# Token rows scattered whole by expert pair, loaded back in plain groups, added into the output; layer norm shifts on GpSimd

## The chip, the cores and the metric

The kernel runs on one core of a Trainium2 chip. The metric is the time of one execution on the device in microseconds (us), median of the runs. Engines are TensorE (PE; PEld is its weight load), VectorE (DVE), ScalarE (ACT), GpSimd (POOL) and SyncE (SP), which here only issues DMAs.

## What is computed

A block of adaptive layer norm, an attention-like recurrence with its own feed-forward, then a mixture of 8 experts of which each token takes 2. Eight sequences of 1,024 tokens, 128 channels, float32:

```
mod = (silu(c) @ wmod)  ->  sa, ca, ga, sb, cb, gb   (128 each, per sequence; |ga|, |gb| >= 0.25)
h = layernorm(x) * (1 + ca) + sa
x = x + ga * attn(h)        # rms norm, 5 mixes, 8-key recurrence S = d*S + k*v, o = r.S, ffn
h = layernorm(x) * (1 + cb) + sb
top 2 of softmax(h @ Wg.T), weights scaled to sum 1
x = x + gb * sum_e weight_e * ((a_e * sigmoid(b_e)) @ Wo + bo)   # a_e, b_e = h @ W1[e] + b1[e]
```

The x of the last line is called x2 below, its h is called h3, and gb the gate.

## The kernel before

**First stage** (`attention_block`). 16 tiles of 512 tokens, two to a sequence, go through a software pipeline: `run_pipeline` runs 27 iterations, and in iteration `it` the function `step` of each engine issues the work of tile `it - lag` for lags 0 to 8. `step` is written out by hand, so its order is the order of the engine's queue. VectorE forms `kv`, eight keys a tile, from `v_spread`, a row spread over the partitions by a DMA of 256 KB (L583), scans it (L1287) and GpSimd multiplies the states by r (L708, eight per tile). Layer norms: VectorE makes mean and variance, GpSimd the variance plus epsilon and the power -1/2 (`rs`, L787 and L789 for the second norm, L806 and L823 for the first), VectorE the shift -mean*rs (`mean_shift`, L1278), and ScalarE h*rs + shift.

**Routing.** After each fourth tile a batch of 16 groups of 128 tokens is routed: on VectorE 30 steps of `Router`, spread over the next iterations, find each token's pair of experts (28 classes) and its place `dest` in a list with a region for each class. Per tile SP stores h3 (L608), x2 (L611) and the gate of the sequence, spread over 512 rows (L619), into `tokens_scratch`. Per group GpSimd scatters rows of 16 bytes, the tags (token number and weights), to `list_scratch` at `dest` (L686). The `spot`s of `list_some` say where in an iteration. `list_scratch` was filled with the tag of no token at the start (`clear_list`). Three batches are listed in the first stage, the fourth in the second. Experts' weights come in iteration 21 (L631), when the state products are done, and are split in two halves on ScalarE and VectorE (L1547, 'gel' and 'w_hi' in rows of this part are reused buffers).

**Second stage** (`expert_block`). After a barrier, 91 groups of 128 places, 46 pairs of groups, 20 groups from the first three batches' full blocks (early) and 71 late. Per group SP loads the tags (L1625, L1626), at a row number read from `row_table`; GpSimd gathers the 128 rows of h3, x2 and gate by token number (L1743, five pairs ahead) and scatters the results (L1749). Per pair TensorE transposes h3 (L1644), multiplies by the class's experts, VectorE multiplies by the gate (`gate`, L1818) and adds x2 (`finish`, L1826). The late groups' loads wait for the last batch's listing (`list_late`), which waits for the early groups' loads.

## Time and profile before

| what | us |
|---|---|
| median of 3 runs (lowest, highest) | 815.12 (813.99, 816.86) |
| the profiled execution's own time | 810.64 |
| its span in the trace | 808.8 |
| busy: TensorE / VectorE | 669.2 / 657.2 |
| busy: ScalarE / GpSimd | 474.8 / 613.5 |

The span runs from the first to the last recorded instruction; 1.8 us of the execution lie around it. An engine's busy time is the sum of its instructions' durations; matmul ends are modelled. The first stage ends at 525.96 us in the trace, the second stage begins at 530.51. A tile is counted by the start of its ruk multiply on VectorE (L1430): 128.37, 152.38, 176.46, 201.36, 225.53, 250.31, 280.82, 310.44, 334.61, 363.10, 398.18, 426.10 us.

### The profile page before, as it was taken

How to read it: one execution, taken by the hardware profiler on the slowest of the kernel's cores; microseconds unless marked ns; L12 is line 12 of the kernel's file. 1: busy time of each engine (PE TensorE's matmuls, PEld its weight loads, DVE VectorE, ACT ScalarE, POOL GpSimd, SP SyncE). 2: the span in 40 equal slices, each digit the busy share in tenths (PEclk: the TensorE clock that was granted, in tenths of full speed). 3: DMA queues.
4: the chain of work that ended last, by engine and by line, in shares of the span. 5: the costliest groups of instructions: out<-in, count | busy, mean ns of one | idle time of the engine just before them, and what ended most of it. 6: DMA issues, size and time to landing. Idle time of an engine off the chain costs nothing. (4 is left out here: it accounts for less than half of the span.)

```text
span 808.8 us, 14121 instructions
## 1 busy us (share of the span) xinstructions
PE 669.2 (83%) x3703; PEld 521.4 (64%) x3703; DVE 657.2 (81%) x1426; ACT 474.8 (59%) x1163; POOL 613.5 (76%) x657
## 2 busy tenths in 40 slices
PE   2566899998999789988877967329879999999993
PEld 0444577676777558665655756118668888888882
DVE  5399999999999999979999467707748887788873
ACT  3664789887997678875655655214334444444441
POOL 5377878998998688999779785636777777777763
PEclk7798999999999899998999977559989999999997
DMA  4987767887887867766774262423144433333320
GB/s 125 244 129 139 125 142 132 130 161 131 157 157 125 127 114 133 128 110 115 100 95 94 63 171 64 95 63 84 32 107 104 97 92 95 97 97 96 97 65 1
DMA packets 95298, 89.64 MB, mean 111 GB/s; under 512 B 22832, under 2 KB 71194, under 8 KB 95094
## 3 DMA queue, kind: packets, MB, share of 16 engines
q1 hardware_dynamic: 84438, 66.49, 45.0%
q0 software_dynamic: 10784, 22.25, 9.9%
q8 instruction: 34, 0.56, 0.3%
q14 instruction: 42, 0.34, 0.1%
HBM read 38.69 MB, written 22.41 MB: 76 GB/s over the span
## 5 line engine op out<-in xcount | busy, mean ns | idle before, releaser
L708 POOL TENSOR_TENSOR rs_prod<-rT,state 128x512 f32<-128x512 f32 x128 | 165.2, 1303 | 35.9 <-DVE state L1287 34.0
L1743 POOL DMA_INDIRECT xg<-tokens_scratch,listed x91 | 88.9, 977 | 42.0 <-issue 25.6
L1749 POOL DMA_INDIRECT out<-res,listed x91 | 91.0, 1000 | 34.6 <-issue 25.7
L1282 DVE TENSOR_TENSOR kv<-key,v_spread 128x512 f32<-128x512 f32 x128 | 84.3, 669 | 10.6 <-DMA v_spread<-vT 9.3
L1713 ACT ACTIVATE sig<-ps_a 128x256 f32<-128x256 f32 x91 | 35.0, 385 | 82.5 <-PE ps_a L1653 69.1
L1287 DVE TENSOR_TENSOR_SCAN state<-decay,state,kv 128x512 f32<-128x512 f32 x64 | 79.9, 1269 | 0.1
L1287 DVE TENSOR_TENSOR_SCAN state<-decay,kv 128x512 f32<-128x512 f32 x64 | 76.0, 1207 | 0.1
L1067 PEld LDWEIGHTS ps_k<-w,gel 128*128 128x128 f32 x512 | 61.0, 199 | 14.7 <-issue 12.5
L1715 ACT ACTIVATE sig<-ps_b 128x256 f32<-128x256 f32 x91 | 35.0, 384 | 51.5 <-PE ps_b L1653 51.5
L1067 PE MATMUL ps_k<-w,gel 128*128 128x128 f32 x512 | 64.0, 285 | 1.2 <-ACT gel L924 1.2
L1790 DVE SCALAR_TENSOR_TENSOR ps_a<-ps_a,listed,sig 128x256 f32<-128x256 f32 x91 | 44.3, 487 | 24.8 <-ACT sig L1713 24.8
L1049 PE MATMUL ps_f<-hnT_hi,mix_hi 128*128 128x512 f32 x128 | 56.4, 440 | 6.5 <-DVE hnT_lo L1411 6.3
L1797 DVE SCALAR_TENSOR_TENSOR half<-ps_b,listed,sig 128x256 f32<-128x256 f32 x91 | 44.0, 483 | 21.8 <-ACT sig L1715 21.4
L686 POOL DMA_INDIRECT list_scratch<-tags,dest x48 | 49.4, 1030 | 11.1 <-issue 9.9
L1051 PE MATMUL ps_f<-hnT_hi,mix_lo 128*128 128x512 f32 x128 | 52.1, 407 | 0.0
L1682 PEld LDWEIGHTS ps_y<-out_w,gT 128*128 128x128 f32 x364 | 47.7, 191 | 6.6 <-issue 1.7
L1050 PE MATMUL ps_f<-hnT_lo,mix_hi 128*128 128x512 f32 x128 | 51.8, 405 | 0.0
L1682 PE MATMUL ps_y<-out_w,gT 128*128 128x128 f32 x364 | 48.2, 275 | 2.2 <-DVE res L1826 1.5
L1034 PE MATMUL ps_o<-rs_prod,reduce_w 128*32 128x512 f32 x256 | 35.8, 633 | 12.9 <-POOL rs_prod L708 12.8
L1650 PE MATMUL ps_a<-bias_all,parts 128*128 x91 | 44.4, 487 | 1.4 <-DVE xT_lo L1785 1.3
L1806 DVE TENSOR_TENSOR glu<-ps_a,half 128x256 f32<-128x256 f32 x91 | 38.2, 419 | 4.3
L1049 PEld LDWEIGHTS ps_f<-hnT_hi,mix_hi 128*128 128x128 f32 x128 | 25.3, 197 | 23.2 <-issue 17.1
(298 smaller groups left out, 2068.4 us busy)
## 6 DMA issues: line engine op xcount, KB each, us to landing
v_spread<-vT SPq DMA_DIRECT2D x128, 256.0 KB, 6.5
xin<-in_L_attn_x SPq DMA_DIRECT2D x16, 256.0 KB, 7.2
tokens_scratch<-mods_scratch SPq DMA_DIRECT2D x16, 256.0 KB, 10.4
x<-in_L_attn_x SPq DMA_DIRECT2D x16, 256.0 KB, 4.8
tokens_scratch<-x SPq DMA_DIRECT2D x16, 256.0 KB, 5.4
tokens_scratch<-h SPq DMA_DIRECT2D x16, 256.0 KB, 4.5
list_scratch<-gel SPq DMA_DIRECT2D x1, 3584.0 KB, 11.9
rs_prod<-in_L_ffn_W SPq DMA_DIRECT2D x8, 256.0 KB, 5.3
```

Of the source, the lines that this page charges most:

```text
L686: pool.indirect_dma_start(list_dram, bass.IndirectOffsetOnAxis(ap=dest[:, g:g + 1], axis=0), tags[:, g, :], None).then_inc(s["listed"], 16)
L708: pool.tensor_tensor(rs_prod[:, p, idx % 4], rT[p][:], state[idx][:, p * NT:(p + 1) * NT], ALU.mult).then_inc(s["rs_ready"], 1)
L1049: pe.matmul(dst[:], mix_hi[:, a, m, :], hnT_hi[p][:, cols_of], start=(a == NOW), stop=False)
L1050: pe.matmul(dst[:], mix_hi[:, a, m, :], hnT_lo[p][:, cols_of], start=False, stop=False)
L1051: mm = pe.matmul(dst[:], mix_lo[:, a, m, :], hnT_hi[p][:, cols_of], start=False, stop=(a == BEFORE))
L1067: mm = pe.matmul(ps_k2[:, q * P:(q + 1) * P], gel[c][:, q * P:(q + 1) * P], w2[:, c, :], start=(c == 0), stop=(c == NF - 1))
L1282: dve.tensor_tensor(kv[idx % 2][:], key[:], v_spread[idx % SPREADS][:], ALU.mult).then_inc(s["kv_ready"], 1)
L1287: dve.tensor_tensor_scan(state[idx][:, 1 + p * NT:1 + (p + 1) * NT], decay[:], kv[idx % 2][:], first, ALU.mult, ALU.add) \
L1650: pe.matmul(dst[:], parts[:], bias, start=True, stop=False)
L1682: mm = pe.matmul(ps_y[:, i * P:(i + 1) * P], gT[k % 2][:, h, i * P:(i + 1) * P], out_w[:, h, :], start=(h == 0), stop=(h == NH2 - 1))
L1743: pool.indirect_dma_start(xg[:, 2 * (k % LOADS) + i, :], None, pay_dram, bass.IndirectOffsetOnAxis(ap=listed[:, j, ID:ID + 1].bitcast(I32) ...
L1749: pool.indirect_dma_start(out_rows, bass.IndirectOffsetOnAxis(ap=listed[:, j, ID:ID + 1].bitcast(I32), axis=0), res[k % RESULTS][:, i, :], ...
```

## The change

* The shift of both layer norms is made on GpSimd: a multiply of the mean by -1, and, behind the power, a multiply by `rs` (both 128x4). VectorE's instruction goes.
* `list_scratch`, its clear and the gates' store go. `sorted_scratch` holds whole rows of 260 floats (h3, gate, tags) by class. For the first two batches SP stages two groups at a time into SBUF (`stage_pair`: h3, gate and tags, three DMAs) and GpSimd scatters them from there (`list_pair`, two scatters at each odd spot, as many as before). For the last two batches the rows lie in `last_rows`, in the memory of the states; `load_last_rows` brings in 3 MB ahead of iteration 20. The third batch's 16 scatters stand at spot 7 in one piece, and the last batch's in the second stage wait for nothing (`list_late`, four a pair).
* x2 is stored to the output, and the second stage's scatter adds to it (`compute_op=ALU.add`); `finish` multiplies by the gate in place of adding x2, and `gate` goes.
* In the second stage SP loads each group's rows itself (`load_group`, no gather). After 12 of them come 28 DMAs that write 128 rows of no token behind the last token of each class (`fill_end`), then the other loads; a pair's loads wait for the results stored six pairs before.
* Wo, the experts' output weights, is loaded in iteration 21 too.

```diff
-    TWO_FOUND, CHOSEN, PLACED, STEPS = 7, 14, 27, 30
+    TWO_FOUND, CHOSEN, TAGGED, PLACED, STEPS = 7, 14, 25, 27, 30
...
-    pay_dram = nc.dram_tensor("tokens_scratch", (TILES * NT + 1, 3 * D), F32, kind="Internal").ap()
-    list_dram = nc.dram_tensor("list_scratch", (CLASSES * STRIDE + P, 4), F32, kind="Internal").ap()
...
+    pay_dram = nc.dram_tensor("tokens_scratch", (EARLY * NT, D), F32, kind="Internal").ap()
+    sorted_dram = nc.dram_tensor("sorted_scratch", (CLASSES * STRIDE + P, ROW), F32, kind="Internal").ap()
...
+        state_rows = keep.enter_context(nc.sbuf_tensor("state_rows", [P, max(DK * (1 + T), 2 * RG * ROW)], F32))
+        last_rows = state_rows[:, 0:2 * RG * ROW].rearrange("p (g c) -> p g c", c=ROW)
...
-                    sp.dma_start(pay_tiles[t, 0], h3[p][:]).then_inc(s["h3_stored"][p], 16)
...
+                        sp.dma_start(pay_tiles[t], h3[p][:]).then_inc(s["h3_stored"][p], 16)
...
+                        sp.dma_start(last_rows[:, (t - early) * NQ + RG:(t - early + 1) * NQ + RG, 0:P], h3[p][:]).then_inc(s["h3_stored"][p], 16)
...
-                    sp.dma_start(pay_tiles[t, 1], x2[p][:]).then_inc(s["x2_stored"][p], 16)
+                    sp.dma_start(out_tiles[t], x2[p][:]).then_inc(s["x2_stored"][p], 16)
...
-                for t, p, b in tile(4):
-                    sp.dma_start(pay_gates[t], mods_dram[b, GB:GB + 1, :].broadcast_to([NT, P])).then_inc(s["gates_stored"], 16)
+                for r in batch(3):
+                    stage_pair(r, 0)
...
                 for t, p, b in tile(3):
                     spread_value(7, t, p)
+                for r in batch(3):
+                    stage_pair(r, 1)
...
+            def stage_pair(r, m):
+
+                if r < LISTED - 1:
+                    first, k = r * RG + 2 * m, m % 2
+                    sp.wait_ge(s["route_step"], r * Router.STEPS + Router.TAGGED)
+                    for p in range(2):
+                        sp.wait_ge(s["h3_stored"][p], 16 * BATCH // 2 * (r + 1))
+                    if r > 0 or m >= 2:
+                        sp.wait_ge(s["listed"][k], 16 * 2 * (r * RG // 4 + m // 2))
+                    sp.dma_start(stage[k][:, :, 0:P], pay_groups[:, first:first + 2, :]).then_inc(s["staged"][k], 16)
+                    sp.dma_start(stage[k][:, :, GATE:TAGS], mods_dram[first * P // (TPB * NT), GB:GB + 1, :].unsqueeze(0).broadcast_to([P, 2, P])) \
+                        .then_inc(s["staged"][k], 16)
+                    sp.dma_start(stage[k][:, :, TAGS:], tags[:, first:first + 2, :]).then_inc(s["staged"][k], 16)
...
+            def load_last_rows():
+
+                sp.wait_ge(s["rs_ready"], TILES * DK)
+                for p in range(2):
+                    sp.wait_ge(s["h3_stored"][p], 16 * (early // 2))
+                sp.dma_start(last_rows[:, 0:RG, 0:P], pay_groups[:, (LISTED - 1) * RG:, :]).then_inc(s["last_staged"], 16)
+                for i in range(2 * BATCH // TPB):
+                    first = i * TPB * NQ
+                    sp.dma_start(last_rows[:, first:first + TPB * NQ, GATE:TAGS],
+                                 mods_dram[early // TPB - BATCH // TPB + i, GB:GB + 1, :].unsqueeze(0).broadcast_to([P, TPB * NQ, P])).then_inc(s["last_staged"], 16)
+
...
+            run_pipeline(step, {CLEAR_AT: store_blank, BIAS_AT + 1: store_bias, ROWS_AT: load_last_rows, EXPERTS_AT: load_experts})
...
+            def list_pair(r, m):
+
+                k = m % 2
+                if r < LISTED - 1:
+                    pool.wait_ge(s["staged"][k], 48 * (r * RG // 4 + m // 2 + 1))
+                    pool.wait_ge(s["route_step"], (r + 1) * Router.STEPS)
+                for n in range(2 * m, 2 * m + 2):
+                    g = r * RG + n
+                    if r < LISTED - 1:
+                        pool.indirect_dma_start(sorted_dram, bass.IndirectOffsetOnAxis(ap=dest[:, g:g + 1], axis=0), stage[k][:, n % 2, :], None).then_inc(s["listed"][k], 16)
+                    else:
+                        pool.indirect_dma_start(sorted_dram, bass.IndirectOffsetOnAxis(ap=dest[:, g:g + 1], axis=0), last_rows[:, n, :], None).then_inc(s["last_listed"], 16)
 
             def list_some(r, spot):
...
+                if r < LISTED - 1 and spot % 2 == 1 and spot <= RG + 1:
+                    list_pair(r, spot // 2 - 1)
+                if r == LISTED - 1 and spot == 7:
+                    pool.wait_ge(s["last_staged"], 16 * (1 + 2 * BATCH // TPB))
+                    pool.wait_ge(s["tags_set"], 1)
+                    pool.wait_ge(s["route_step"], LISTED * Router.STEPS)
+                    for m in range(RG // 2):
+                        list_pair(r, m)
+
+            def mean_shift(dst, rs, done):
+
+                pool.tensor_tensor(dst[:], dst[:], rs[:], ALU.mult).then_inc(done, 1)
...
+                    after(pool, s["xn4_ready"], t - 1)
+                    pool.tensor_scalar(shift4[:], mv4[:, :, 0], -1.0, 0.0, ALU.mult, ALU.add)
                     pool.tensor_scalar(ve4[:], mv4[:, :, 1], 1.0, EPS_LN, ALU.mult, ALU.add).then_inc(s["ln2_ve"], 1)
                     after(pool, s["ln2_ve"], t)
                     pool.tensor_tensor(rs4[:], ve4[:], minus_half[:], ALU.pow).then_inc(s["ln2_rstd"], 1)
+                    after(pool, s["ln2_rstd"], t)
+                    mean_shift(shift4, rs4, s["shift2_ready"])
...
-                    after(dve, s["ln1_rstd"], t)
-                    mean_shift(shift1, mv1, rs1, s["shift1_ready"])
...
+            dve.tensor_copy(end_table[:], off[0:1, :, RG:RG + 1].rearrange("p e g -> p (e g)"))
...
+            def load_group(j):
+                k = j // 2
+                if k >= LOADS and j % 2 == 0:
+                    sp.wait_ge(s["stored"][(k - LOADS) % RESULTS], 16 * count_to(k - LOADS, RESULTS))
+                row = sp.value_load(row_table[0:1, j:j + 1], min_val=0, max_val=CLASSES * STRIDE)
+                sp.dma_start(xg[:, slot(j), :], sorted_dram[bass.ds(row, P), :]).then_inc(s["x_in"][k % LOADS], 16)
+
+            def fill_end(c):
+
+                row = sp.value_load(end_table[0:1, c:c + 1], min_val=0, max_val=CLASSES * STRIDE)
+                sp.dma_start(sorted_dram[bass.ds(row, P), :], sorted_dram[CLASSES * STRIDE:, :]).then_inc(s["filled"], 16)
+
+            for j in range(2 * LOADS):
+                load_group(j)
+                if j == 1:
+                    sp.dma_start(out_b[:], ins["L0_ffn_bo"].unsqueeze(0).broadcast_to([P, P])).then_inc(s["small_in"], 16)
+            for c in range(CLASSES):
+                fill_end(c)
+            for j in range(2 * LOADS, GROUPS):
+                if j == early_groups:
 
                     sp.wait_ge(s["listed"], 16 * RG)
-                load_list(c)
+                    sp.wait_ge(s["filled"], 16 * CLASSES)
+                load_group(j)
...
             def scatter(k, i):
                 j = 2 * k + i
                 pool.wait_ge(s["res_ready"], k + 1)
-                pool.indirect_dma_start(out_rows, bass.IndirectOffsetOnAxis(ap=listed[:, j, ID:ID + 1].bitcast(I32), axis=0), res[k % RESULTS][:, i, :], None,
-                                        bounds_check=TILES * NT - 1, oob_is_err=False).then_inc(s["stored"][k % RESULTS], 16)
+                pool.indirect_dma_start(out_rows, bass.IndirectOffsetOnAxis(ap=share_of(j, ID).bitcast(I32), axis=0), res[k % RESULTS][:, i, :], None,
+                                        bounds_check=TILES * NT - 1, oob_is_err=False, compute_op=ALU.add).then_inc(s["stored"][k % RESULTS], 16)
 
             def list_late(first, end):
...
                     g = LATE_BATCH + n
-                    pool.indirect_dma_start(list_dram, bass.IndirectOffsetOnAxis(ap=dest[:, g:g + 1], axis=0), tags[:, g, :], None).then_inc(s["listed"], 16)
-
...
+                    pool.indirect_dma_start(sorted_dram, bass.IndirectOffsetOnAxis(ap=dest[:, g:g + 1], axis=0), last_rows[:, RG + n, :], None).then_inc(s["listed"], 16)
+
             for k in range(PAIRS):
-                if k + AHEAD < PAIRS:
-                    gather(k + AHEAD, 0)
+                if k < LIST_AT:
+                    list_late(RG * k // LIST_AT, RG * (k + 1) // LIST_AT)
                 if k >= 1:
                     scatter(k - 1, 0)
-                if k + AHEAD < PAIRS and members(k + AHEAD) == 2:
-                    gather(k + AHEAD, 1)
-                if k >= 1:
                     scatter(k - 1, 1)
-                if k < LIST_AT:
-                    list_late(RG * k // LIST_AT, RG * (k + 1) // LIST_AT)
...
+            def finish(k):
...
-                y = ps_y[:, 0:n * P].rearrange("p (i d) -> p i d", i=n)
-                dve.tensor_tensor(y, y, xg[:, slot:slot + n, 2 * P:3 * P], ALU.mult).then_inc(s["gated"], 1)
...
-                dve.wait_ge(s["gated"], k + 1)
...
-                dve.tensor_tensor(res[k % RESULTS][:, 0:n], y, xg[:, slot:slot + n, P:2 * P], ALU.add).then_inc(s["res_ready"], 1)
+                dve.tensor_tensor(res[k % RESULTS][:, 0:n], y, xg[:, first:first + n, GATE:TAGS], ALU.mult).then_inc(s["res_ready"], 1)
```

The order of GpSimd in one listing tile (middle of an iteration; `ve`, `rs` are the norms' scalars, `rs_prod` the state products), before:

```order
L787 TENSOR_SCALAR ve<-mv 128x4
L789 TENSOR_TENSOR rs<-ve,minus_half 128x4
L708 TENSOR_TENSOR rs_prod<-rT,state 128x512
L686 DMA list_scratch<-tags,dest 229504x4
L806 TENSOR_SCALAR ve<-mv 128x4
L708 TENSOR_TENSOR rs_prod<-rT,state 128x512
L686 DMA list_scratch<-tags,dest 229504x4
L823 TENSOR_TENSOR rs<-ve,minus_half 128x4
```

and of the change:

```order
L842 TENSOR_SCALAR shift<-mv 128x4
L843 TENSOR_SCALAR ve<-mv 128x4
L845 TENSOR_TENSOR rs<-ve,minus_half 128x4
L757 TENSOR_TENSOR shift<-shift,rs 128x4
L761 TENSOR_TENSOR rs_prod<-rT,state_rows 128x512
L865 TENSOR_SCALAR shift<-mv 128x4
L866 TENSOR_SCALAR ve<-mv 128x4
L761 TENSOR_TENSOR rs_prod<-rT,state_rows 128x512
L740 DMA sorted_scratch<-stage,dest 233088x260 x2
L883 TENSOR_TENSOR rs<-ve,minus_half 128x4
L757 TENSOR_TENSOR shift<-shift,rs 128x4
```

Four small operations are added per tile, and two scatters stand together where there was one and one.

The order of SP in the same tile, from the store of x2 on, before:

```order
L611 DMA tokens_scratch<-x 128x4x128
L583 DMA v_spread<-vT 128x1x512
L617 DMA x<-in_L_attn_x 128x4x128
L619 DMA tokens_scratch<-mods_scratch 512x128
L583 DMA v_spread<-vT 128x1x512 x3
L516 DMA mods_late<-mods_scratch 128x384
```

and of the change:

```order
L618 DMA out<-x 128x4x128
L586 DMA v_spread<-vT 128x1x512
L624 DMA x<-in_L_attn_x 128x4x128
L656 DMA stage<-tokens_scratch 128x2x128
L657 DMA stage<-mods_scratch 128x2x128
L659 DMA stage<-tags 128x2x4
L586 DMA v_spread<-vT 128x1x512
L656 DMA stage<-tokens_scratch 128x2x128
L657 DMA stage<-mods_scratch 128x2x128
L659 DMA stage<-tags 128x2x4
L586 DMA v_spread<-vT 128x1x512 x2
L523 DMA mods_late<-mods_scratch 128x384
```

Six staging DMAs with their waits stand around the spread of key 7 and ahead of those of keys 0 and 1; the gates' store is gone.

SP in the second stage, one list load before:

```order
L1625 TENSOR_LOAD row_table
L1625 ISA x2
L1626 ISA
L1626 DMA listed<-list_scratch 128x4
```

and of the change the twelfth group load and the first fill:

```order
L1690 ISA
L1690 DMA xg<-sorted_scratch 128x260
L1694 TENSOR_LOAD end_table
L1694 ISA x2
L1695 ISA
L1695 DMA sorted_scratch<-sorted_scratch 16x2080
```

A load or a fill has the same five instructions as a list load had; 28 fills stand between loads 12 and 13.

## Rows read from the trace of the kernel before

**Rows 1.** the page, busy us by engine (share of the span)

```profile
PE 669.2 (83%) x3703; PEld 521.4 (64%) x3703; DVE 657.2 (81%) x1426; ACT 474.8 (59%) x1163; POOL 613.5 (76%) x657
```

**Rows 2.** four stretches: start:end, length, busy PE PEld DVE ACT POOL, clock, DMA, GB/s

```profile
128.40:250.30 121.90, 116.05 (x702) 87.99 (x701) 120.08 (x229) 106.83 (x262) 112.93 (x111) 0.99 0.81 145
250.30:310.40 60.10, 50.12 (x278) 38.12 (x277) 60.00 (x121) 41.38 (x108) 45.68 (x44) 0.91 0.72 119
310.40:440.00 129.60, 110.44 (x641) 81.25 (x639) 123.97 (x217) 91.33 (x219) 112.72 (x107) 0.95 0.69 116
...
598.40:788.20 189.80, 189.80 (x1081) 162.54 (x1080) 152.87 (x397) 86.57 (x216) 143.59 (x145) 1.00 0.36 94
```

**Rows 3.** grouped instructions, 100 to 450 us

```profile
L1278 DVE SCALAR_TENSOR_TENSOR shift<-mv,rs 128x4 f32<-128x4 f32 x23 | 14.3, 621 | 4.2 <-POOL rs L789 4.2
...
L789 POOL TENSOR_TENSOR rs<-ve,minus_half 128x4 f32<-128x4 f32 x12 | 12.3, 1022 | 1.0
...
L787 POOL TENSOR_SCALAR ve<-mv 128x4 f32<-128x4 f32 x12 | 3.0, 249 | 1.0
```

**Rows 4.** GpSimd in order of time, one calm tile (start, length, what)

```profile
201.80 1.29 POOL L757 TENSOR_TENSOR h_all<-h_all,mods_early 128x512 f32<-128x512 f32 x1 [1.34 <-ACT h_all L860]
...
210.44 0.19 POOL L782 TENSOR_SCALAR ve<-ssq 128x4 f32<-128x4 f32 x1 [0.81 <-ACT hn L855]
...
213.06 1.29 POOL L708 TENSOR_TENSOR rs_prod<-rT,state 128x512 f32<-128x512 f32 x1
...
225.78 1.30 POOL L757 TENSOR_TENSOR h_all<-h_all,mods_early 128x512 f32<-128x512 f32 x1
```

**Rows 5.** VectorE in order of time, first stage: waits and shifts

```profile
32.09 0.87 DVE L1267 BATCH_NORM_STATS2 st<-xin 128x6 f32<-128x128 f32 x4 [7.20 <-DMA xin<-in_L_attn_x]
...
213.30 1.07 DVE L1278 SCALAR_TENSOR_TENSOR shift<-mv,rs 128x4 f32<-128x4 f32 x1
...
350.55 1.24 DVE L1278 SCALAR_TENSOR_TENSOR shift<-mv,rs 128x4 f32<-128x4 f32 x1 [4.16 <-POOL rs L789]
```

**Rows 6.** one listing tile in order of time: GpSimd, sync queue, VectorE

```profile
340.18 1.28 POOL L759 TENSOR_TENSOR h_all<-h_all,mods_early 128x512 f32<-128x512 f32 x1
...
341.23 3.46 SPq L583 DMA_DIRECT2D v_spread<-vT  x3
...
356.79 1.26 DVE L1282 TENSOR_TENSOR kv<-key,v_spread 128x512 f32<-128x512 f32 x2
```

**Rows 7.** DMA issues on the page: KB each, us to landing

```profile
v_spread<-vT SPq DMA_DIRECT2D x128, 256.0 KB, 6.5
...
list_scratch<-gel SPq DMA_DIRECT2D x1, 3584.0 KB, 11.9
```

**Rows 8.** all engines in order of time, the first stage's last tiles

```profile
465.76 7.25 SPq L631 DMA_DIRECT2D rs_prod<-in_L_ffn_W  x8
...
468.18 0.96 POOL L686 DMA_INDIRECT list_scratch<-tags,dest  x1 [0.30 <-issue]
...
470.56 1.28 ACT L865 ACTIVATE h<-h_all,rs 128x128 f32<-128x128 f32 x4 [3.28 <-POOL rs L779]
```

**Rows 9.** sync queue and GpSimd at the second stage's start

```profile
530.51 3.73 SPq L1626 DMA_DIRECT2D listed<-list_scratch  x4
...
535.47 17.25 SPq L1626 DMA_DIRECT2D listed<-list_scratch  x16
535.75 0.99 POOL L1743 DMA_INDIRECT xg<-tokens_scratch,listed  x1 [13.53 <-DMA listed<-list_scratch]
```

**Rows 10.** TensorE's transposes of a pair's rows, one row a pair

```profile
540.29 0.66 PE L1644 MATMUL ps_t<-ident,xg 128*128 128x128 f32 x2 [14.90 <-DMA xg<-tokens_scratch,listed]
...
590.89 0.69 PE L1644 MATMUL ps_t<-ident,xg 128*128 128x128 f32 x2 [6.82 <-DMA xg<-tokens_scratch,listed]
...
598.36 0.38 PE L1644 MATMUL ps_t<-ident,xg 128*128 128x128 f32 x2
```

**Rows 11.** grouped instructions, 530.5 us to the end

```profile
L1818 DVE TENSOR_TENSOR ps_y<-ps_y,xg 128x256 f32<-128x256 f32 (+1 forms) x46 | 19.7, 429 | 1.6
```

More of the change, by code:

```diff
@@ L33 @@
 GATE_MIN = 0.25
-ID, LOW, HIGH, BOTH = range(4)
+ID, LOW, HIGH, BOTH, TAG = range(5)
+GATE, TAGS, ROW = P, 2 * P, 2 * P + TAG
 PACK = 1 << 12
```

188 lines of the change are left out of this document (83 added, 105 removed).

## The prediction

> **What bounds the kernel now.** I read the page's busy shares first, then the stretches, then each engine in order of time where two engines meet. By the page TensorE (83%) and VectorE (81%) are near each other and GpSimd stands at 76% [rows 1], but these are averages. By the stretches the first stage belongs to VectorE: in the five calm tiles it is busy 120.08 of 121.9 us, and GpSimd 112.93 [rows 2], so a tile takes 24.4 us. In the two tiles in which a batch is routed VectorE is busy 60.00 of 60.10 us, 30.05 a tile, and GpSimd only 45.68: there a VectorE instruction taken away is time won. In the four tiles and a half with listing the two are nearly level (123.97 and 112.72 of 129.6). The second stage's steady part, 598.4 to 788.2, is TensorE's alone: 189.80 of 189.80 us, 36 pairs, so 5.27 us a pair; nothing done to VectorE, GpSimd or the gathers shows there. What is left are the joints: start, end of the first stage, start of the second.
>
> All sums are against the profiled execution's 810.64 us. The median is 4.5 us above it and the lowest run 3.4; I carry the difference over unchanged.
>
> **The change, part by part.**
>
> *Start.* The clear of 3,584 KB, 11.9 us from issue to landing [rows 7], goes. VectorE waits 7.20 us for the first x until 32.09 [rows 5], while the clear shares the DMA engines. Not all of the wait is the clear's, and TensorE's first work hangs on weights too. I take **-1.5**, bounds 0 and -3.
>
> *Shift, VectorE's side.* 23 shifts from 100 to 450 us take 14.3 us, 0.62 each, with 4.2 us of waits for GpSimd's power [rows 3]; one a tile for each norm is 1.24 us less a tile.
> The short ones are long where GpSimd runs beside them: the one at 213.30 took 1.07 us beside the state product at 213.06 that took 1.29 [rows 4, 5]. The Trainium skill, "SBUF — State Buffer", section "Who interferes with whom", says that a VectorE instruction with two SBUF inputs contends with a GpSimd instruction that reads SBUF; by that rule, with which this row agrees, 128x4 can cost as much as what stands beside it.
>
> *Shift, GpSimd's side.* Two operations a norm. The 128x4 tensor_scalar is 0.249 us [rows 3]. A 128x4 multiply of two tensors doesn't occur; it lies between this and the power of the same size, 1.022 us. A multiply is nearer to the tensor_scalar than to a power, so a norm costs about 0.5 us and a tile **1.0** more (1.0 to 2.5). GpSimd's calm tile, from the same instruction at 201.80 to that at 225.78, has one idle time of 0.81 us [rows 4], so its need is some 23.2 of 24.0 us; it becomes 24.2. VectorE's need becomes 24.0-1.2 = 22.8. The tile then goes by GpSimd, at 24.2 against 24.4 now: GpSimd's gaps are used up and VectorE's gain is not seen. Five calm tiles: **0**; bounds -6 (1.2 x 5, if the longer operations shrink with the contention) and +6 (1.2 us a tile, if the multiply costs as the power).
> The skill has a rule that speaks against this part: "Perfetto Trace Analysis", section "Optimizing Scalar/DVE Operations", says that GPSIMD and DVE share a port, "so offloading operations between those two might not help". By it all shift terms would be 0, the sum -5.3 in place of -7.3.
>
> *Two routing tiles.* There GpSimd has room, (60.10-45.68)/2 = 7.2 us a tile, and VectorE is full. Two shifts a tile, 4 x 0.62 = 2.5, of which some is given back by waits: **-2** (0 to -2.5).
>
> *Listing tiles.* Scatters stay as many. The shift's wait of 4.16 us at 350.55 [rows 5] stood at the head of VectorE's queue; without it scans go on, but GpSimd is the engine that was late, and it gets 1 us more a tile. Against that SP's queue: it had the spreads of keys 7, 0 and 1 out from 341.23 on [rows 6]. Now the second staging waits for scatters that stand behind GpSimd's instruction at 340.18 (end 341.46). Two scatters at 1.27 [rows 8] end at about 344; with some 2.4 us of landing and three DMAs the spreads of keys 0 and 1 go out at about 350, in place of about 342.4. A spread lands in 6.5 us [rows 7], so at 356.5, and VectorE takes key 0 at 356.79 [rows 6]: just in time. I put +2 for the queue against -2 for the shift: **0**, bounds -6 and +10.
>
> *First stage's end.* The scatters ahead of the last tile's rms norm are two fewer: the third batch's stood one by one at 1.26 us each (0.96 and 0.30 of issue), and ScalarE waited 3.28 us for the `rs` behind them until 470.56 [rows 8]. That is **-2.5**. The other 14 become 16 in one piece at a spot where TensorE, ScalarE and VectorE split the experts' weights, as 14 did. What can turn it: 3 MB of rows are loaded ahead of h3's and x2's stores, x and the experts' weights. These weights are 2 MB in 7.25 us [rows 8], so 3 MB take 11 to 12. They are issued an iteration before the weights, at about 440. I take them as hidden behind the last tile's recurrence; without that cover +10. Bounds -4, +10.
>
> *Second stage's start.* Before: four list loads from 530.51, gathers from 535.75 [rows 9], first transpose at 540.29 [rows 10]. Now loads 0 and 1 go out at 530.5 and 531.6 and land some 2.4 us later: first transpose at 534.1, **-6.2**. Pairs 0 to 5 have their rows in xg. Pair 6 has its loads behind the fills. A load with a row number read takes SP (17.25-3.73)/12 = 1.13 us [rows 9], and a fill has the same instructions. The second load of pair 6 is the 42nd such DMA: out at 530.5+41x1.13+0.4 = 577.2, landed at 579.3. TensorE would reach it at 534.1+6x5.27 = 565.7. It stalls 13.6 us, and some 2.2 more go on a lowered clock after it, as behind the stall of 6.82 us at 590.89: 7.47 us from that pair to 598.36, against 5.27 [rows 10]. So the tenth pair begins at 579.3+3x5.27+2.2 = 597.3, against 598.36: **-1.0** in all. The old losses (58.07-9x5.27 = 10.6 us) are replaced by this one. The late rows are scattered by 560 and the fills landed by 580; the late loads' wait at group 20, some 7 DMAs on, isn't felt.
>
> *Steady part and tail.* `gate` goes, 46 x 0.429 [rows 11], under TensorE: 0. In the tail the last one counts, -0.4 and its hand-over -0.4; the adding scatter, which reads its target, +0.5: **-0.3**.
>
> Sum: -1.5+0-2+0-2.5-1-0.3 = **-7.3**, so 803.3 in the profile and about 808 in the median.
>
> **The rivals.**
> A (the forecast): 808, own range 804 to 812.5. Chance 0.45.
> B: the fills don't hold the loads (SP issues a DRAM-to-DRAM DMA of 16 rows much faster than 1.13 us; at 0.7, 12 us are saved). For: 16x2080 is fewer pieces than 128x260. Against: the load of the row number stands before each. With both stalls gone -1.0 becomes some -15.8, 792 to 794. Chance 0.10.
> C (slower): SP's queue in order is the new wait. Staging waits for landed scatters with the spreads of keys 0 and 1 behind it. It decides once these go out over 1 us later than 350; each of the eight staging tiles then stops VectorE by 1.5 to 2.5 us, +12 to +20, or the 3 MB push the experts' weights, +10. Centre 820. For: the slack worked out above is 0.3 us. Against: part of the eight tiles' VectorE waits on GpSimd anyway. Chance 0.20.
> D (slower): GpSimd bounds the calm tiles. If the multiply costs as the power (1.0 against 0.25, twice a tile) its need is 25.7, 1.3 us over, in 10 to 12 tiles: +13 to +16 on -2 less, 821. It decides from a multiply of 0.4 us on. Against: the multiply isn't a power. Chance 0.10.
> E: gains and losses cancel, 813 to 817.5, chance 0.15: by the skill's rule on the shared port, with half of C's price.
>
> **How the numbers follow.** What this kernel's measurement tells from no change is about 0.3%, 2.4 us. The time is A's. The range of 799 to 822 holds A, E, and the greater part of C and D, and leaves out B and the far ends. Faster: A (0.45), B (0.10) and a few hundredths of the mildest C: 0.58. Same: 0.15. Slower: C and D without that: 0.27.
>
> **What would show it.** A calm tile within 0.4 us of 24.4, with GpSimd idle under 0.5 us in it and VectorE waiting for products or powers; the 128x4 multiply under 0.4 us. Routing tiles near 29. First transpose at 3.6 us behind the second stage's first SP instruction; one stall at the seventh pair of 12 to 15 us on xg's load, none at the ninth. Steady pairs at 5.27. Wrong it is if the spreads of keys 0 and 1 become VectorE's longest waits in listing tiles, if the multiply is near 1 us, or if pair 6 doesn't stall.

## The result, and the profile after

The changed kernel takes **844.54 us** (median of 4 runs, 841.78 to 844.82) against 814.56 for the kernel before (4 runs): the ratio is 1.037, 95% interval 1.0343 to 1.0397. It is slower by 3.7%, where 808 was forecast. The profiled run took 844.45 us, 33.8 more than before's 810.64. One of the four runs of e6 below took 930.01 us at a granted clock of 0.724, where its others had 0.903 to 0.905, and is left out of its figures.

The page's head and busy times, which answer to [rows 1]:

```profile
span 842.7 us, 14259 instructions
...
PE 667.4 (79%) x3703; PEld 521.3 (62%) x3703; DVE 626.0 (74%) x1349; ACT 473.3 (56%) x1163; POOL 573.5 (68%) x631
```

All engines are less busy and the span is 33.9 us longer, so the loss is waiting. Cut at the same marks in both traces (ruk multiplies, the second stage's first DMA, TensorE's first transposes of pairs 1 and 10; pairs are counted from 1 here, so the prediction's pair 6 is pair 7):

| stretch | before | after | difference | forecast |
|---|---|---|---|---|
| to the fifth tile's ruk | 128.37 | 129.08 | +0.7 | -1.5 |
| five calm tiles | 121.94 | 114.78 | -7.2 | 0 |
| two routing tiles | 60.13 | 59.92 | -0.2 | -2 |
| listing tiles, to the last ruk | 115.66 | 111.36 | -4.3 | 0 |
| last ruk to the second stage's first DMA | 104.41 | 142.49 | **+38.1** | -2.5 |
| from there to pair 1 | 9.78 | 3.95 | -5.8 | -6.2 |
| pair 1 to pair 10 | 58.07 | 69.55 | **+11.5** | +5.2 |
| pair 10 to the end | 210.44 | 211.57 | +1.1 | -0.3 |

The stretches of after (columns as in [rows 2]):

```profile
129.00:243.80 114.80, 113.62 (x702) 86.41 (x698) 114.63 (x219) 105.41 (x261) 109.12 (x129) 1.00 0.93 142
243.80:303.80 60.00, 49.41 (x292) 36.56 (x288) 59.79 (x118) 43.60 (x110) 48.33 (x55) 0.97 0.74 111
303.80:415.10 111.30, 98.43 (x568) 73.73 (x560) 104.56 (x188) 81.54 (x195) 98.29 (x106) 0.95 0.84 146
...
446.60:492.40 45.80, 25.26 (x140) 19.98 (x138) 11.42 (x36) 15.98 (x38) 12.38 (x14) 0.77 0.65 110
...
631.10:820.60 189.50, 189.50 (x1082) 162.35 (x1081) 140.45 (x361) 86.51 (x216) 111.89 (x72) 1.00 0.41 68
```

From 446.6 to 492.4 VectorE works 11 and GpSimd 12 of 46 us while the DMA engines are 65% busy. The sync queue in order of time (start, length, what) says with what:

```profile
446.60 0.76 SPq L666 DMA_DIRECT2D state_rows<-tokens_scratch  x1
447.40 24.80 SPq L669 DMA_DIRECT2D state_rows<-mods_scratch  x4
472.31 7.08 SPq L523 DMA_DIRECT2D mods_late<-mods_scratch  x1
...
492.44 9.86 SPq L679 DMA_DIRECT2D rs_prod<-in_L_ffn_W  x8
...
557.63 1.53 SPq L1690 DMA_DIRECT2D xg<-sorted_scratch  x2
...
572.04 36.82 SPq L1695 DMA_DIRECT2D sorted_scratch<-sorted_scratch  x28
609.62 202.01 SPq L1690 DMA_DIRECT2D xg<-sorted_scratch  x79
```

Four loads of gate rows, 2 MB, hold SyncE for 24.80 us, 3.4 times as long as the 2 MB of experts' weights in [rows 8] (7.25 us), and the DMA behind them for 7.08 more (4.55 in e1, which has no gate rows). The weights go out at 492.44, 77.3 us after the last ruk; before it was 465.76, 39.7 after it. GpSimd in the same stretch, and the two ends at the barrier:

```profile
495.39 1.05 POOL L740 DMA_INDIRECT sorted_scratch<-stage,dest  x1 [35.08 <-DMA stage<-tags]
...
547.98 0.96 POOL L742 DMA_INDIRECT sorted_scratch<-state_rows,dest  x1 [0.30 <-issue]
...
549.71 0.21 DVE L1624 TENSOR_SCALAR pair_table<-ps_m 1x71 int32<-1x71 f32 x1
556.70 0.17 DVE L1877 MEMSET parts_f<- 128x128 f32 x1 [6.79 <-PEq L55]
```

GpSimd waits 35.08 us for a staging DMA that stands in SyncE's queue behind the gate rows. At the barrier VectorE's tables end at 549.92, and the second stage starts on VectorE at 556.70 (6.8 us behind; before 3.6): what ends last now is most likely GpSimd's last scatter of the 16, issued at 547.98, and its landing. TensorE's transposes, one row a pair, against [rows 10]:

```profile
561.58 0.66 PE L1718 MATMUL ps_t<-ident,xg 128*128 128x128 f32 x2 [12.23 <-DMA xg<-sorted_scratch]
...
587.06 0.38 PE L1718 MATMUL ps_t<-ident,xg 128*128 128x128 f32 x2
...
612.87 0.69 PE L1718 MATMUL ps_t<-ident,xg 128*128 128x128 f32 x2 [20.39 <-DMA xg<-sorted_scratch]
...
620.60 0.38 PE L1718 MATMUL ps_t<-ident,xg 128*128 128x128 f32 x2
...
631.13 0.38 PE L1718 MATMUL ps_t<-ident,xg 128*128 128x128 f32 x2
```

Pair 7 waits 20.39 us for its load behind the fills. The adding scatter, and the gate rows' landing (KB each, us to landing):

```profile
L1814 POOL DMA_INDIRECT out<-res,xg x91 | 141.7, 1557 | 116.4 <-DVE res L1875 98.6
...
state_rows<-mods_scratch SPq DMA_DIRECT2D x4, 512.0 KB, 25.6
```

### The profile page after: what moved, and what is told of

It reads as the page before. It is cut to its first block and busy times, and to the rows that moved or that the text cites. A ratio compares the mean times of both kernels' runs of the same rounds, so it can differ in the third digit from the quotient of the medians.

```text
span 842.7 us, 14259 instructions
## 1 busy us (share of the span) xinstructions
PE 667.4 (79%) x3703; PEld 521.3 (62%) x3703; DVE 626.0 (74%) x1349; ACT 473.3 (56%) x1163; POOL 573.5 (68%) x631
## 5 line engine op out<-in xcount | busy, mean ns | idle before, releaser
L1814 POOL DMA_INDIRECT out<-res,xg x91 | 141.7, 1557 | 116.4 <-DVE res L1875 98.6
L761 POOL TENSOR_TENSOR rs_prod<-rT,state_rows 128x512 f32<-128x512 f32 x128 | 151.3, 1195 | 33.1 <-DVE state_rows L1353 31.6
L1353 DVE TENSOR_TENSOR_SCAN state_rows<-decay,state_rows,kv 128x512 f32<-128x512 f32 x64 | 79.9, 1270 | 0.2
L1353 DVE TENSOR_TENSOR_SCAN state_rows<-decay,kv 128x512 f32<-128x512 f32 x64 | 76.1, 1209 | 0.2
L1852 DVE SCALAR_TENSOR_TENSOR half<-ps_b,xg,sig 128x256 f32<-128x256 f32 x91 | 44.0, 484 | 38.1 <-ACT sig L1789 38.1
L1136 PEld LDWEIGHTS ps_k<-w,gel 128*128 128x128 f32 x512 | 62.0, 202 | 13.9 <-issue 11.7
L740 POOL DMA_INDIRECT sorted_scratch<-stage,dest x32 | 33.5, 1047 | 50.9 <-DMA stage<-tags 44.1
L1845 DVE SCALAR_TENSOR_TENSOR ps_a<-ps_a,xg,sig 128x256 f32<-128x256 f32 x91 | 44.4, 488 | 23.4 <-ACT sig L1787 23.3
L929 ACT ACTIVATE h<-x,shift,rs 128x128 f32<-128x128 f32 x64 | 26.2, 480 | 40.3 <-POOL shift L757 40.3
L1718 PE MATMUL ps_t<-ident,xg 128*128 128x128 f32 x91 | 18.0, 279 | 32.6 <-DMA xg<-sorted_scratch 32.6
```

What stands on the lines that cost most here:

```text
L761: pool.tensor_tensor(rs_prod[:, p, idx % 4], rT[p][:], state[idx][:, p * NT:(p + 1) * NT], ALU.mult).then_inc(s["rs_ready"], 1)
L1136: mm = pe.matmul(ps_k2[:, q * P:(q + 1) * P], gel[c][:, q * P:(q + 1) * P], w2[:, c, :], start=(c == 0), stop=(c == NF - 1))
L1353: dve.tensor_tensor_scan(state[idx][:, 1 + p * NT:1 + (p + 1) * NT], decay[:], kv[idx % 2][:], first, ALU.mult, ALU.add) \
L1814: pool.indirect_dma_start(out_rows, bass.IndirectOffsetOnAxis(ap=share_of(j, ID).bitcast(I32), axis=0), res[k % RESULTS][:, i, :], None, b ...
L1845: dve.scalar_tensor_tensor(out=ps_a[j % 2][:, 0:HE], in0=ps_a[j % 2][:, 0:HE], scalar=share_of(j, LOW), in1=sig[j % 2][:, 0], op0=ALU.mult ...
L1852: dve.scalar_tensor_tensor(out=half[j % 2][:], in0=ps_b[j % 2][:, 0:HE], scalar=share_of(j, HIGH), in1=sig[j % 2][:, 1], op0=ALU.mult, op1 ...
```

## The experiments

Times are comparable within a group only, since groups ran on different chips; each has its own time for the kernel before. The change itself ran beside 814.56 us for the kernel before, in none of the groups; where the first group is set against it, 1.4 us of the difference may be the chip's. How a time splits into tiles and stages comes from one trace of each kernel.

### First group (before: 813.18 us)

**e1.** The four loads are taken out:

```diff
                 sp.dma_start(last_rows[:, 0:RG, 0:P], pay_groups[:, (LISTED - 1) * RG:, :]).then_inc(s["last_staged"], 16)
-                for i in range(2 * BATCH // TPB):
-                    first = i * TPB * NQ
-                    sp.dma_start(last_rows[:, first:first + TPB * NQ, GATE:TAGS],
```

> The changed kernel without the four loads that spread the gate rows into the last two batches' rows (L669, 2 MB; the gates of these tokens are left out, zeros or states stand in their place; 120 columns are cleared at the start in exchange). Theory Q (the loads hold SyncE's queue, with the second batch's staging and the experts' weights behind them): the sync queue is free at 448 in place of 472 us, GpSimd's wait of 35 us for staging shrinks to under 6, the experts' weights are issued near 457 in place of 492, and the kernel takes 36 us less, 806 to 812. Theory S (the staging itself, its waits in the sync queue, costs the time; the gate rows only lie beside it): at most 10 us less, 834 to 840.

Measured: 812.94 us, ratio 0.999 (0.9969 to 1.0011), about 32 less than the change and 1 us above theory Q's range. The four loads are the loss: from the last ruk to the second stage's first DMA it is 112.3 us in place of 142.5, and GpSimd waits for staging 5.3 us at most in place of 35. The weights go out at 462.67, 48.2 us after the last ruk, so 8.5 us more than before remain ahead of them.

**e2.** The same four loads, other source:

```diff
-                                 mods_dram[early // TPB - BATCH // TPB + i, GB:GB + 1, :].unsqueeze(0).broadcast_to([P, TPB * NQ, P])).then_inc(s["last_staged"], 16)
+                                 pay_groups[:, i * TPB * NQ:(i + 1) * TPB * NQ, :]).then_inc(s["last_staged"], 16)
```

> The changed kernel, with the four 512 KB loads reading stored h3 rows, all different, in place of one gate row 1,024 times over; as many pieces of 512 bytes, to the same places (so the gates of the last two batches are wrong numbers). If the number of pieces sets their time: the four still take 24 to 25 us of the sync queue and the kernel 843 to 846. If reading one row again and again is what makes them slow: four take 10 to 14 us, at the rate of the 1 MB load ahead of them, and the kernel is 10 to 15 us faster, 830 to 835.

Measured: 819.43 us, ratio 1.0075 (1.0049 to 1.0101), 25 less than the change, where I had expected 10 to 15. The sync queue and, last, the landing of the four:

```profile
444.02 0.76 SPq L666 DMA_DIRECT2D state_rows<-tokens_scratch  x1
444.82 10.74 SPq L669 DMA_DIRECT2D state_rows<-tokens_scratch  x4
...
465.73 10.44 SPq L679 DMA_DIRECT2D rs_prod<-in_L_ffn_W  x8
...
state_rows<-tokens_scratch SPq DMA_DIRECT2D x4, 512.0 KB, 8.3
```

As many pieces of 512 bytes to the same places take 10.74 us of the queue in place of 24.80, and land in 8.3 us in place of 25.6. What is slow is 1,024 reads of the same 512 bytes, not the number or size of pieces. The gain is larger than the 14 us of queue, since what stands behind the loads is quicker too: the experts' weights go out 52.8 us after the last ruk in place of 77.3.

**e3.** Only the place:

```diff
-            run_pipeline(step, {CLEAR_AT: store_blank, BIAS_AT + 1: store_bias, ROWS_AT: load_last_rows, EXPERTS_AT: load_experts})
+            run_pipeline(step, {CLEAR_AT: store_blank, BIAS_AT + 1: store_bias, EXPERTS_AT: load_experts, EXPERTS_AT + 1: load_last_rows})
```

> The changed kernel with the 3 MB load moved from ahead of iteration 20 to ahead of iteration 22, behind the second batch's staging and the experts' weights; nothing is left out. Theory Q: staging and weights go out as in the kernel before, the third batch's 16 scatters wait for the rows instead; these end by 500 us, when the scatters would start, so 30 us or more come back, 808 to 818. If the transfer's traffic and not its place in the queue costs the time: 835 to 845.

Measured: 840.42 us, ratio 1.0317 (1.0286 to 1.0348).

```profile
462.63 8.65 SPq L679 DMA_DIRECT2D rs_prod<-in_L_ffn_W  x8
...
481.19 27.45 SPq L669 DMA_DIRECT2D state_rows<-mods_scratch  x4
...
553.99 1.54 SPq L1690 DMA_DIRECT2D xg<-sorted_scratch  x2
```

and on GpSimd, at the head of the third batch's scatters:

```profile
524.98 1.05 POOL L742 DMA_INDIRECT sorted_scratch<-state_rows,dest  x1 [28.32 <-DMA state_rows<-mods_scratch]
```

Here my theory missed, and the time lies in the range that I had given to traffic. The trace shows a plainer reason. The experts' weights were out at 462.63, as in e1, and still only 4 us came back: the loads took 27.45 us from 481.19 on, GpSimd waited 28.32 us for them until 524.98, and the third batch's 16 scatters (20 us) and the barrier come behind. The queue's order chooses who waits; the slow reads cost the time in either place, since their rows are needed before the stage can end.

**e4.** The kernel before, and only the shifts on GpSimd:

```diff
+                    pool.tensor_scalar(shift4[:], mv4[:, :, 0], -1.0, 0.0, ALU.mult, ALU.add)
                     pool.tensor_scalar(ve4[:], mv4[:, :, 1], 1.0, EPS_LN, ALU.mult, ALU.add).then_inc(s["ln2_ve"], 1)
...
+                    mean_shift(shift4, rs4, s["shift2_ready"])
```

> The kernel before with the layer norm shifts alone moved to GpSimd. By the trace of the change, whose five calm tiles took 22.96 us each in place of 24.38 and whose tiles with listing took 4 us less in all, this part is worth 8 to 11 us: 804 to 807. By the prediction's sum (0 in calm tiles, -2 in routing tiles, -2 in listing tiles, -1 at the end) it is worth 5: 810. By the rule that the two engines share a port: 0, 815.

Measured: 817.97 us, ratio 1.005 (1.003 to 1.0071): slower, which none of the three had. The waits of VectorE from 128 to 430 us (us in total, times, longest):

```profile
DVE kv L1290 <- DMA v_spread<-vT: 5.5, 5, 2.0
```

VectorE was busy 116.13 in place of 120.08 of the calm 121.9 us, and waited for spreads, 5.5 us against 1.8 before, all in the calm tiles. Calm tiles took 24.26 us against 24.38. The last ruk stands at 432.99, 6.9 us later than before; 4.8 of these are in the listing tiles (120.4 us against 115.7), where no spread is waited for, but ScalarE's `sd_g` (3.6 us, once) and TensorE's `ps_k` (2.1, once) are.

### Second group (before: 910.06 us)

On this chip the kernel before, and the two that are built on it, took 908 to 910 us, some 97 more than the kernel before on the first; e5's trace has its first stage at the old times (last ruk at 426.58 us) and its loss in the second. Of e5 and e7 I therefore read the first stage.

**e5 and e7.** Before, and before with the shifts on GpSimd, both with

```diff
-                    sp.dma_start(pay_gates[t], mods_dram[b, GB:GB + 1, :].broadcast_to([NT, P])).then_inc(s["gates_stored"], 16)
+                    sp.dma_start(pay_gates[t], ins["L0_attn_x"].rearrange("b t d -> (b t) d")[t * NT:(t + 1) * NT, :]).then_inc(s["gates_stored"], 16)
```

> The kernel before with the gates' store (L619, 256 KB a tile) reading 512 different rows of x in place of one gate row 512 times (the second stage multiplies by wrong numbers). Theory H, that one row read again and again is what makes such a DMA slow: it lands in 3 to 5 us in place of 10.4, and spreads that share the queue land sooner. VectorE is still full with its shifts, so the time moves little: 809 to 814. If the number of pieces makes it slow: it lands in 10 us and the time is that of before, 813.

> The kernel before with both: shifts on GpSimd and the gates' store reading rows of x (wrong numbers for the gate). Theory I, that the two parts need each other (shifts free VectorE, and without a quick store the spreads of v are then waited for): 803 to 808, calm tiles near 23, VectorE waiting under 1 us for v_spread from 128 to 430 us, where it waited 5.5 with the shifts alone. Rival, that the shift loses by GpSimd's load or the shared port: 815 to 818, as the shifts alone.

Measured: 909.94 (ratio 0.9996, 0.9961 to 1.003) and 908.36 us (0.9998, 0.9965 to 1.0032). Alone, a store from many rows leaves calm tiles at 24.07 us and the last ruk at 426.58 (before 426.10); no spread is waited for any more, and they land in 5.1 us in place of 6.5. The page has no landing for the store itself. With the shifts moved it gives 23.56 and 428.89, against 24.26 and 432.99 with the shifts alone, and the waits for spreads of 5.5 us are gone. So theory I holds in its direction for the calm tiles, and fails for the whole: both together are 2.8 us behind the kernel before at the last ruk. The listing tiles take 120.3 us, as in e4, with the waits for `sd_g` (3.5) and `ps_k` (2.1) still there, so spreads are not what lengthens them once the shifts are on GpSimd. What does was not tried.

**e6.** The change with both shifts back on VectorE:

```diff
-                    pool.tensor_scalar(shift4[:], mv4[:, :, 0], -1.0, 0.0, ALU.mult, ALU.add)
...
-                    mean_shift(shift4, rs4, s["shift2_ready"])
...
+                    after(dve, s["ln2_rstd"], t)
+                    mean_shift(shift4, mv4, rs4, s["shift2_ready"])
```

> The changed kernel with the two shifts back on VectorE as before. If moving them is what shortened the calm tiles from 24.38 to 22.96 us once the gates' store had left the queue: tiles are back at 24.2 and the kernel takes 8 to 14 us more, 852 to 858. If the store's going alone shortened them: tiles stay near 23 and the time at 844.

Measured: 849.95 us, the median of three runs; the change itself was not timed on this chip. Calm tiles are 23.64 us against 22.96, half of what the first case said, but the last ruk stands at 414.75, against 415.14: routing tiles (59.0 against 59.9), listing tiles (109.8 against 111.4) and the start (127.75 against 129.08) give back what the calm ones gain. The start's part is no effect of the edit: two traces of f1 have it at 126.45 and 128.41.

**f1.** The change mended: four loads of 64 KB, then copies on VectorE.

```diff
+                for i in range(2 * BATCH // TPB):
+                    sp.dma_start(gate_in[:, i, :], mods_dram[early // TPB - BATCH // TPB + i, GB:GB + 1, :].broadcast_to([P, P])).then_inc(s["gates_in"], 16)
...
+                    dve.tensor_copy(last_rows[:, first:first + TPB * NQ, GATE:TAGS],
+                                    gate_in[:, i, :].unsqueeze(1).broadcast_to([P, TPB * NQ, P])).then_inc(s["gates_set"], 1)
```

> The changed kernel, complete in what it computes: the gates of the last two batches come in by four loads of 64 KB (128 pieces each in place of 1,024) into a buffer that is free by then, and VectorE copies each into the rows of 8 groups, four copies of 128x1024 of about 1.1 us, at the start of iteration 21. Expected near the run without these gate rows (812.9), plus up to 4 us of copies on the path: 812 to 818. If reads of one row cost by their number wherever they stand, the 512 left cost about 3 us of the 25.

Measured: 819.38 us, 30.6 less than e6 on the same chip and 1 above the range. The four small loads hold the queue for 2.03 us and the four copies take 2.56. The second stage starts at 524.46 in its trace, but group loads and fills are slower on this chip:

```profile
527.45 13.76 SPq L1700 DMA_DIRECT2D xg<-sorted_scratch  x10
541.98 43.01 SPq L1705 DMA_DIRECT2D sorted_scratch<-sorted_scratch  x28
```

Ten loads take 13.76 us, where the change took 10.89 on the other chip, and the fills 43.01 against 36.82.

### Third group (before: 919.1 us)

**f1 again, f2, f3, e8.** f2 spreads the fills between the loads (edit below), f3 also has e6's edit, e8 is f2 without `compute_op=ALU.add` on the result scatters:

```diff
-            for c in range(CLASSES):
-                fill_end(c)
+            SPREAD = {4: 2, 6: 3, 8: 3, 10: 3, 12: 3, 14: 3, 16: 3, 18: 3, 20: 5}
```

> The kernel with the gates copied once more, as the base for the next three on one chip: the chip of its first run took 910 us for the kernel before, whose second stage alone had changed (13.8 us for ten group loads in place of 10.8, in the kernel with the copies). With loads at 1.09 us as in the other runs: 806 to 813.

> The same, and the 28 fills spread between the early groups' loads (two ahead of load 4, three ahead of each pair's loads from 6 to 18, five ahead of load 20) in place of 28 in a row behind load 11. If the fills in a row are what holds pair 6: the stall of 20 to 24 us there is gone; the fills still have to land before load 20, 20 loads and 28 fills are 59 us of queue against 53 us of pairs, so a stall of 5 to 10 us remains at pair 10, and 12 to 16 us come back. If the fills' own transfers hold the loads by traffic: the same 20 us are lost in pieces, and the time stays.

> The same with the shifts back on VectorE. From the traces the calm tiles get 0.7 us longer each (23.64 with the shifts on VectorE, 22.96 without) and the last tile's ruk multiply was as early in both (414.75 and 415.14): no difference to f2 within 2 us. By the calm tiles alone it would be 3 to 4 us slower, by the shifts-alone run (817.97 against 813.18) 4 us faster.

> The kernel with the fills spread (f2), its result scatters writing in place of adding (x2 is left out of the output). The adding scatter takes GpSimd 1.557 us each against 1.000 before. In the steady part TensorE hides it; at the end three stand in a row, so 1.2 to 1.7 us come back and nothing else; if adding slows other DMAs by its reads (steady pairs, group loads), more than 3.

Measured: 821.12, 810.88, 813.14 and 814.89 us; ratios to the kernel before on this chip 0.8943 (0.8913 to 0.8972), 0.8827 (0.8791 to 0.8863), 0.8853 (0.8822 to 0.8884) and 0.887 (0.8833 to 0.8907). f1 missed its 806 to 813: ten group loads took 13.43 us here too. Spreading gives 10.2 us back, in place of 12 to 16; TensorE's longest wait for a group's rows behind the first pair is 3.65 us, where f1's is 18.89. The shifts on GpSimd are worth 2.3, inside the intervals. The plain scatter took 0.983 us in place of 1.558, and from the last result to the last scatter's start 1.8 us in place of 3.3, yet the whole was 4 us slower, with intervals that overlap: the adding costs nothing that this measurement can find.

### Fourth group (before: 811.02 us)

**f4.** Eight fills at the end of the first stage:

```diff
+            for c in range(FILLED_EARLY):
+                row = sp.value_load(end_table[0:1, c:c + 1], min_val=0, max_val=CLASSES * STRIDE)
+                sp.dma_start(sorted_dram[bass.ds(row, P), :], sorted_dram[CLASSES * STRIDE:, :]).then_inc(s["filled_early"], 16)
```

**e9 and e10.** f2 with the gates' store put back ahead of the staging, reading one row (e9) or rows of x (e10):

```diff
+                for t, p, b in tile(4):
+                    sp.dma_start(spare_dram[t * NT:(t + 1) * NT, :], mods_dram[b, GB:GB + 1, :].broadcast_to([NT, P])).then_inc(s["spare_stored"], 16)
```

> The kernel with copied gates and spread fills once more, as the base of the next three. On the chip of its first run the kernel before took 919 us and this one 810.9. On a chip like that of the first four runs (before 813) its group loads should go out at 1.09 us in place of 1.34 and it should take 800 to 806; on one like the second 809 to 813.

> The same with the first eight fills issued by SyncE at the end of the first stage, as soon as VectorE has the classes' ends, and 20 spread as before. SyncE is idle there for 28 us and the ends are known 12 us ahead of the second stage, so eight fills at 1.3 to 1.5 us fit with their landing; the remaining stalls at the pairs before the late groups shrink by up to 8 x 1.3 = 10 us. Expected 5 to 10 us less than the base; 0 or more time if the first stage's end then waits for these fills.

> The base with the gates' store put back into each tile's queue as it stood before (256 KB from one row, to a spare buffer that nobody reads). If this store is what made the tiles of the kernel before longer: calm tiles go from 22.8 back to 24 us or more, the last tile's ruk multiply from 415 to 425 or later, and the kernel takes 8 to 14 us more. If the gain of the first stage came from elsewhere (clear, x2 to the output, order): 0 to 3 us.

> The same store of 256 KB, reading 512 different rows of x in place of the gate row. If reading one row again and again makes it costly, as in the load of the last rows: this one costs under a third of what the store from one row costs. If its 256 KB of writes and its place in the queue do: as much.

| kernel | us | ratio to before |
|---|---|---|
| f2 again | 800.11 | 0.9862 (0.9826 to 0.9898) |
| f4 | 796.91 | 0.9828 (0.9801 to 0.9855) |
| e9 | 823.27 | 1.0157 (1.0118 to 1.0197) |
| e10 | 805.87 | 0.9927 (0.9903 to 0.995) |

A store that nobody reads costs 23.2 us when it reads one row 512 times a tile, where I had expected 8 to 14, and 5.8 when it reads 512 rows. Of the 23.2, 11.1 are there at the last ruk and 10 more come up to the second stage's first DMA (546.50 against 525.24). e9's waits of VectorE, and its DMAs with KB and us to landing:

```profile
DVE kv L1353 <- DMA v_spread<-vT: 14.1, 9, 3.1
...
v_spread<-vT SPq DMA_DIRECT2D x128, 256.0 KB, 6.8
...
spare_scratch<-mods_scratch SPq DMA_DIRECT2D x16, 256.0 KB, 10.4
```

and e10's:

```profile
DVE kv L1353 <- DMA v_spread<-vT: 2.3, 2, 1.5
...
v_spread<-vT SPq DMA_DIRECT2D x128, 256.0 KB, 5.8
...
spare_scratch<-in_L_attn_x SPq DMA_DIRECT2D x16, 256.0 KB, 5.3
```

With e9 the last ruk is at 424.31, calm tiles take 23.96 us and the listing tiles 117.6; with e10 it is 414.58, 22.96 and 111.3, and without either store (f2) 413.20, 22.95 and 111.1. f4, the best of all, is 1.7% faster than the kernel before and 3.2 us faster than f2, with intervals that overlap, where 5 to 10 were expected. From pair 1 to pair 13 it takes 67.2 us in place of 74.2, but its second stage starts 2.6 us later: VectorE waits at the barrier for 10.19 us in place of 6.70, most likely for the fills. Its sync queue around the barrier:

```profile
513.30 10.10 SPq L688 DMA_DIRECT2D sorted_scratch<-sorted_scratch  x8
527.88 1.50 SPq L1706 DMA_DIRECT2D xg<-sorted_scratch  x2
```

## Why the prediction was wrong

**The first stage's end: the step that failed.** I priced the 3 MB ahead of iteration 20 by the experts' weights, 2 MB in 7.25 us, "so 3 MB take 11 to 12", hid them "behind the last tile's recurrence" and put +10 as the far bound; it was +38.1. The 1 MB of h3 did land in 9.3 us. The 2 MB of gates read four rows 1,024 times each, and each of the four loads took 25.6 us to land. e1 shows that they are 32 us of the time (30 of the 38.1), e2 that 25 of these are their single source row. The row that would have warned of them stood on the page of before, among the DMA issues (KB each, us to landing):

```profile
tokens_scratch<-mods_scratch SPq DMA_DIRECT2D x16, 256.0 KB, 10.4
...
tokens_scratch<-x SPq DMA_DIRECT2D x16, 256.0 KB, 5.4
tokens_scratch<-h SPq DMA_DIRECT2D x16, 256.0 KB, 4.5
```

A store of 256 KB from one row landed in 10.4 us, stores of as much from SBUF in 5.4 and 4.5. It was the nearest row by source, and I took the nearest by size. Cover was counted for the transfer, not for who stood behind it: GpSimd, 35 us, and the weights.
Some 8.5 us between the last ruk and the weights are left without the gate rows (e1), and the whole stretch is 7.9 us longer than before, where I had -2.5. Staging in SyncE's queue ahead of the weights is a likely cause (in e1 GpSimd still waits for it four times there, 14.6 us in all), and 3.2 us at the barrier are most likely GpSimd's 16 scatters in one piece, for which my sum had nothing; neither was tried alone.

**Calm tiles: size and reason off.** Forecast 0 because GpSimd would need 24.2 us. It needed less, and VectorE still set the tile, busy 114.63 of 114.80 us where GpSimd was busy 109.12: the 128x4 multiply took 0.203 us, where I put 0.25 and more, and the products shrank. The rows are of the change's calm tiles, then the products of the whole run of before and of e6, and last e6's shifts from 100 to 440 us, against [rows 3]:

```profile
L761 POOL TENSOR_TENSOR rs_prod<-rT,state_rows 128x512 f32<-128x512 f32 x39 | 45.6, 1184 | 1.2 <-DVE state_rows L1353 0.8
...
L757 POOL TENSOR_TENSOR shift<-shift,rs 128x4 f32<-128x4 f32 x10 | 2.0, 203 | 0.8
...
L708 POOL TENSOR_TENSOR rs_prod<-rT,state 128x512 f32<-128x512 f32 x128 | 165.2, 1303 | 35.9 <-DVE state L1287 34.0
...
L757 POOL TENSOR_TENSOR rs_prod<-rT,state_rows 128x512 f32<-128x512 f32 x128 | 151.6, 1194 | 42.3 <-DVE state_rows L1345 40.9
...
L1336 DVE SCALAR_TENSOR_TENSOR shift<-mv,rs 128x4 f32<-128x4 f32 x23 | 10.9, 473 | 2.3 <-POOL rs L839 2.3
```

(columns: busy, mean ns, idle before.) So the tile went to 22.96 us, near the 22.8 that I had put down as VectorE's need. But the shift's move earned only 0.7 of the 1.4 us a tile (e6), and 0.1 where spreads of v share the queue with a slow store (e4). The rest has two parts, and my sum had a term for neither; only its bound of -6, which -7.2 passed, was for operations that shrink. Some 0.4 us a tile are waits for spreads (1.8 us in five tiles), which go with the store from one row (e5). Some 0.3 are the shifts themselves: in e6, still on VectorE, one takes 0.473 us in place of 0.621, beside products of 1,194 ns in place of 1,303. The products are short in all kernels built on the change, e9 with the store put back too (1,187), and long in e5 (1,301) and e4 (1,302), so neither the shift's move nor the store shortens them. Which part of the change does stays open.

**Listing tiles, start, routing.** Listing tiles gained 4.3 us, of my terms -2 and +2. The change without the shifts gained 5.8 (e6), so it isn't the shift's move. By e9 it is the store from one row: put back into f2, it lengthens the listing tiles from 111.1 to 117.6 us, and by 11.1 us in all at the last ruk. But in the kernel before, the same store reading many rows gave nothing there (e5: 117.5 us against 115.7). Why it costs the changed kernel more stays open. The clear's going gave nothing that can be seen: the fifth tile's ruk stands at 128.37 before and at 126.45 to 129.64 in the traces without the clear. The routing tiles did not gain 2 us, though VectorE was full: 59.79 busy of 60.00 with two operations fewer a tile.

**Second stage.** The start was right (-5.8 for -6.2), and so was the stall's place and mechanism. The term that was mis-sized is a fill's time: 28 fills and the gap to load 13 took 37.6 us (572.04 to 609.62), 1.34 each and not 1.13, and the stall 20.4 in place of 13.6. f2 shows that the fills in a row are the stall by moving them (-10.2 us). Rival B is out: a fill took longer than a load, not less.

**Rivals.** C, a sync queue in order as the new wait, was the right family, 0.20. Its first half, +12 to +20 from staging, did not occur: VectorE waited 0.5 us for spreads from 128 to 430 us. Its second half, the 3 MB pushing the weights by 10, is what happened, at more than three times the price. D did not occur. Two of my sums are off, without moving the forecast: without any shift term the sum is -3.3 and not -5.3, since the listing tiles' -2 is one too, and rival B's term is -16.8 and not -15.8. The Trainium skill's rule of the shared port ("Perfetto Trace Analysis", "Optimizing Scalar/DVE Operations") would make the shift worth 0. In the changed kernel it is worth 0 at the last ruk (e6) to 2.3 us (f3 against f2), and in the kernel before it costs 5, so the rule did better than my -2 in the routing tiles. But what took the gain back in e4's calm tiles was a wait for spreads of v, which is no port, and in its listing tiles waits for ScalarE and TensorE, whose cause was not tried.

## What to carry to other kernels

Price a transfer by the nearest row with the same **source pattern**, not the same size: one DRAM row read over and over is slow (a load of 512 KB landed in 25.6 us here, in 8.3 from different rows in pieces of the same 512 bytes), and it is cheaper to bring the row in once per partition and copy it on an engine (f1: 2.03 us of queue and 2.56 us of copies in place of 24.80 us of queue). Before a long transfer is put into an in-order queue, list who stands behind it and who waits for the result; moving it to another place helps only if neither is on the path. An engine freed by moving work is a gain only once the next supplier, in e4's calm tiles the spreads of v, keeps up.

## What the runs showed that I had not expected

Reads of one 512-byte row slow down their neighbours: e9's store raised the landing of v's spreads from 5.8 us (e10) to 6.8 and VectorE's waits for them from 2.3 to 14.1 us.

Chips differ in the second stage of the kernel before: it took 811 to 815 us on those of the first and fourth groups and the first timing, 910 and 919 on those of the second and third. In e5's trace GpSimd waits for results before it may gather the next rows:

```profile
POOL xg L1743 <- DVE res L1826: 84.7, 21, 9.6
```

That is 84.7 us in 21 waits from 598 us on, with the first stage unchanged. The kernels with plain group loads differ by 11 us between such chips (f2: 800.11 and 810.88). So on the third group's chip f2 is 11.7% faster than the kernel before, and on the fourth's 1.4%; what differs between the chips the traces don't tell.
